# Expert rows placed as they come and read back in order, the first expert tiles begun before the last batches are routed, and an end in five chunks

## What is computed

```python
h = layernorm(x) * (1 + ca) + sa
x = x + ga * attention(h)          # 16 heads of 8, band of +-128 tokens
h = layernorm(x) * (1 + cb) + sb
logits = h @ gate                  # 8 experts
w, e = softmax over the two largest logits
x = x + gb * sum_k w[k] * ((silu(h @ w1[e[k]]) * (h @ w3[e[k]])) @ w2[e[k]])
```

## Time and profile before

| | us |
|---|---|
| median of three runs | 348.94 |
| the runs | 348.21 to 350.21 |
| the profiled execution | 349.13 |
| its span | 347.3 |
| TensorE busy | 277.7 |
| VectorE busy | 227.4 |
| ScalarE busy | 184.9 |
| GpSimd busy | 180.6 |
| mean granted clock of TensorE | 0.917 |

### The profile page before, as it was taken

One profiled execution on the slowest core, in us unless ns is written; L12 is line 12 of the kernel. 1 busy time (PEld: TensorE's weight loads), 2 busy tenths in 40 slices (PEclk: granted clock), 3 DMA queues, 4 the chain that ended last, 5 costly groups with the idle time before them and its releaser, 6 DMA issues. The chain is left out here.

```text
span 347.3 us, 6884 instructions
## 1 busy us (share of the span) xinstructions
PE 277.7 (80%) x2281; PEld 204.6 (59%) x2281; DVE 227.4 (65%) x573; ACT 184.9 (53%) x406; POOL 180.6 (52%) x269
## 2 busy tenths in 40 slices
PE   3568799999998999999854056999999999999200
PEld 2134354555554555555333035999999999999200
DVE  5657978888888799887437893555555555554064
ACT  7432477757675766667710104556665555555050
...
DMA packets 36243, 26.89 MB, mean 77 GB/s; under 512 B 4088, under 2 KB 31752, under 8 KB 36208
## 3 DMA queue, kind: packets, MB, share of 16 engines
...
## 5 line engine op out<-in xcount | busy, mean ns | idle before, releaser
L819 DVE TENSOR_REDUCE negm<-psA 128x4 f32<-128x1024 f32 x64 | 78.2, 1223 | 14.2 <-PE psA L1141 13.1
L428 ACT ACTIVATE probs<-psB 128x512 f32<-128x512 f32 x128 | 71.1, 593 | 21.4 <-PE psB L1163 21.1
L589 POOL TENSOR_SCALAR_AFFINE_SELECT probs<-probs 128x512 f32<-128x512 f32 x64 | 39.1, 634 | 42.2 <-ACT probs L428 42.2
L700 POOL DMA_INDIRECT y_d<-kd,sca_idx x39 | 45.3, 1162 | 22.9 <-ACT kd L497 22.9
L1297 PE MATMUL psA<-kd,probs 128*128 128x128 f32 x416 | 53.1, 284 | 0.0
L1297 PEld LDWEIGHTS psA<-kd,probs 128*128 128x128 f32 x416 | 51.1, 201 | 0.0
L1138 PE MATMUL psA<-kd,qs 96*128 96x512 bf16 x128 | 47.6, 395 | 1.7 <-DVE negm L819 1.5
L695 POOL DMA_INDIRECT kd<-h_d,gat_idx x39 | 38.2, 980 | 18.5 <-PE psO L1289 9.8
L1163 PE MATMUL psB<-qs,kd 98*128 98x256 bf16 x256 | 45.1, 273 | 1.5 <-ACT probs L428 1.0
L1307 PE MATMUL psM<-probs,kd 128*128 128x128 f32 x312 | 41.3, 275 | 0.4 <-ACT kd L497 0.4
L1307 PEld LDWEIGHTS psM<-probs,kd 128*128 128x128 f32 x312 | 37.9, 192 | 0.6 <-DVE kd L1030 0.6
...
## 6 DMA issues: line engine op xcount, KB each, us to landing
...
probs<-y_d SPq DMA_DIRECT2D x8, 256.0 KB, 5.0
h_d<-h SPq DMA_DIRECT2D x8, 128.0 KB, 1.9
out_dram<-probs SPq DMA_DIRECT2D x4, 256.0 KB, 2.3
...
```

The costliest lines, as they stand in the source:

```text
L428: nc.scalar.activation(probs[:, kt, n % PRING], psB[:, kt, :].rearrange("p (h q) -> p h q", h=H2), ACT.Exp).then_inc(s["exped"], 1)
L589: nc.gpsimd.affine_select(out=u, in_=u, compare_op=ALU.is_ge, fill=0.0, base=0, pattern=[[0, 2 * H2], [-sign, P]], channel_multiplier=sign ...
L700: pool.indirect_dma_start(y_d, bass.IndirectOffsetOnAxis(ap=sca_idx[:, n:n + 1], axis=0), ys[:, r], None).then_inc(scattered[r], 16)
L819: nc.vector.tensor_reduce(negm[:, b % 2, :, :, j], psA[:, n % 2].rearrange("p q (h k) -> p q h k", h=H2), AX.X, ALU.max, negate=True).then ...
```

## The change

- Every expert has a region of rows in DRAM (xs_d), as large as it could need. The place of a row is its rank within its expert plus the region's start, so it is known as soon as the ranks of its batch are. VectorE computes it per batch (`place_rows`), and GpSimd writes the rows there (`put_rows`, four indirect writes a batch, 520 bytes a row: 128 channels, the row of y_d that the result goes to, and its weight). A copy of h2 for the second choice is made by a transfer (`copy_h2`). Selection matrices, the inversion and the gathers are gone.
- Rows never written are blanks; they are written once at the start, only in front of each region and in a few dummy tiles (`fill_blanks`).
- The tile list is made in two parts. The first 13 of the 39 tiles (NEARLY) are full tiles of rows from batches 0 to 4 (EB = 5), since at least so many exist for any split; `early_list` is made in step 8. The other 26 come from `late_list`, made between tiles 5 and 6.
- SyncE loads a tile's rows with one plain transfer (`load_xs`, a ring of five) and w2 of the tile's expert straight from its input (`load_w2`, a ring of three), each behind a register read. The resident array of w2 and its copies on VectorE are gone. Rings for up products are two instead of three; results have a ring of six.
- The steps end with step 8. The tail of batches 5 to 7 stands between the tiles 0 to 5, on each engine.
- ScalarE applies the row's weight while it copies the result. The end has five chunks (4, 4, 4, 2, 2 tiles of tokens); SyncE loads first choices and ScalarE's queue second ones, 2 KB or 1 KB a partition; VectorE alone adds, gates and adds x.

```diff
...
+    XRING = 5
+    PAYRING = 3
+    ENDS = (0, 4, 8, 12, 14, 16)
+    YRING = 6
+    W = C + 2
+    EB = 5
+    NEARLY = -(-(TOPK * L * EB - E * (P - 1)) // P)
...
+            def load_w2(n):
+
+                if n >= TRING:
+                    sp.wait_ge(s["y_ps"], n - TRING + 1)
+                e = sp.value_load(tile_e[0:1, bass.ds(n, 1)], min_val=0, max_val=E - 1)
+                sp.dma_start(w2_t[:, n % TRING].rearrange("p (k c) -> p k c", c=C),
+                             w2[bass.ds(e, 1)].rearrange("e (k p) c -> p (e k) c", p=P)).then_inc(w2_in[n % TRING], 16)
+
...
+                if n >= XRING:
+                    sp.wait_ge(*result_down(n - XRING))
+                row = sp.value_load(tile_row[0:1, bass.ds(n, 1)], min_val=0, max_val=XROWS - P)
+                sp.dma_start(xs[:, n % XRING], xs_d[bass.ds(row, P), :]).then_inc(xs_in[n % XRING], 16)
...
+            sp.wait_ge(s["list_ready"], 2)
+            sp.wait_ge(s["scoresB"], 2 * NPAIR * B)
+            for n in range(TRING):
+                load_w2(n)
+            for done, count in xs_put_by(EB):
+                sp.wait_ge(done, count)
+            for n in range(XRING):
+                load_xs(n)
+            copy_h2(B - 2)
+            for n in range(NTILE):
+                if n + TRING < NTILE:
+                    if n + TRING == NEARLY:
+                        sp.wait_ge(s["list_ready"], 4)
+                    load_w2(n + TRING)
+                if n + XRING < NTILE:
+                    if n + XRING == NEARLY:
+                        sp.wait_ge(s["list_ready"], 4)
+                        sp.wait_ge(s["blanked"], 32)
+                        for done, count in xs_put_by(B):
+                            sp.wait_ge(done, count)
+                    load_xs(n + XRING)
+                if n == 2:
+                    copy_h2(B - 1)
+
+            for n in range(NTILE - YRING, NTILE):
+                sp.wait_ge(*result_down(n))
+            for i, (lo, hi) in enumerate(zip(ENDS, ENDS[1:])):
+                sp.dma_start(y01[:, 0, lo:hi], y_t[:, 0, lo:hi]).then_inc(y_in[i], 16)
...
+            def y_copy(n):
                 act.wait_ge(s["y_ps"], n + 1)
-                if not first(turn):
-                    act.wait_ge(scattered[r], 16 * turn)
-                nc.scalar.copy(ys[:, r], psY).then_inc(s["y_ready"], 1)
...
+            for i, (lo, hi) in enumerate(zip(ENDS, ENDS[1:])):
+                act.dma_start(y01[:, 1, lo:hi], y_t[:, 1, lo:hi]).then_inc(y_in[i], 16)
...
+            def put_rows(b, k, t):
+
+                r = b % PAYRING
+                pool.wait_ge(s["dest_ready"], 3 * b + 3)
+                if k == 1:
+                    pool.wait_ge(h2_copied[r], 16 * (b // PAYRING + 1))
+                pool.indirect_dma_start(xs_d, bass.IndirectOffsetOnAxis(ap=dest[:, b, k, t:t + 1], axis=0),
+                                        pay[:, r, k, t], None).then_inc(xs_put[r], 16)
...
                 for j in range(NPAIR):
+                    if 5 <= step < B and j >= 4:
...
                     if j == 3 and has(step - 3):
                         ln2_rstd(step - 3)
                     if j == 1 and has(step - 3) and step - 3 < B - 1:
...
+            put_rows(3, 1, 1)
+            put_rows(4, 0, 0)
+            pad_term(B - 1)
+            put_rows(4, 0, 1)
+            x1_sum(B - 2)
+            put_rows(4, 1, 0)
+            ln2_rstd(B - 2)
+            put_rows(4, 1, 1)
+            h2_scale(B - 2)
+            h2_shift(B - 2)
             for n in range(NTILE):
...
+                if n == 5:
+                    weights_pow(B - 1)
+                    put_rows(B - 3, 1, 1)
+                if n == 6:
+                    put_rows(B - 2, 0, 1)
+                if n == 7:
+                    put_rows(B - 2, 1, 1)
+                if n == 8:
+                    put_rows(B - 1, 0, 1)
+                if n == 9:
+                    put_rows(B - 1, 1, 1)
                 scatter(n)
-
-            for i in range(3):
-                tt = slice(NT // 4 * i, NT // 4 * (i + 1))
-                pool.wait_ge(s["comb_ready"], i + 1)
-                nc.gpsimd.tensor_tensor(outb[:, tt], comb[:, tt], x_sb[:, tt], ALU.add).then_inc(s[f"out_ready{i}"], 1)
+                if n == 4:
+                    put_rows(B - 3, 1, 0)
+                if n == 5:
+                    put_rows(B - 2, 0, 0)
+                if n == 6:
+                    put_rows(B - 2, 1, 0)
+                if n == 7:
...
+            def place_rows(b):
+
+                dve.wait_ge(s["rank_ps"], b + 1)
+                if b >= 2:
+                    dve.wait_ge(s["dest_ready"], 3 * b - 3)
+                nc.vector.tensor_tensor(
+                    picked[:, b % 2], pick[:, :, 2 * b:2 * b + 2],
+                    rank_at(b).rearrange("p (o t e) -> p o t e", o=1, e=E).broadcast_to([P, TOPK, 2, E]), ALU.mult).then_inc(s["rank_read"], 1)
+                nc.vector.tensor_copy(pay[:, b % PAYRING, :, :, C:C + 1].rearrange("p k t o -> p k (t o)").bitcast(I32),
...
+            def early_list():
+
+                dve.wait_ge(s["count_ps"], 1)
+                up_to(0, count_at(EB - 1))
+                list_done(nc.vector.tensor_scalar(jump[:], upto[:, 0, E:], -float(P), float(CAP), ALU.mult, ALU.add))
+                tile_list(0, NEARLY, jump[:])
...
+                    if j == 0 and step == B:
+                        place_rows(3)
+                        logits_copy(4)
+                    if j == 2 and step == B:
+                        top2(4)
+                    if j == 4 and step == B:
+                        place_rows(4)
+                        early_list()
...
+            w1_copy(1, 1)
+            ln2_stats(B - 2)
+            normalise_attn(B - 1)
+            ln2_normalise(B - 2)
...
-            n = NT // 4
-            for i in range(4):
...
-                dve.wait_ge(s[f"y_in{i}"], 32)
-                for j in range(n * i, n * i + n):
-                    dve.wait_ge(s["y0_scaled"], j + 1)
-                    ins = nc.vector.scalar_tensor_tensor(out=comb[:, j], in0=y01[:, 1, j], scalar=wts[:, 3, j:j + 1], in1=y01[:, 0, j],
-                                                         op0=ALU.mult, op1=ALU.add)
-                step_done(ins)
+                    if n + 2 == NEARLY:
+                        dve.wait_ge(s["list_ready"], 4)
+                    w1_copy(n + 2, (n + 2) % TRING)
+                if n == 1:
+                    gate_attn(B - 1)
+                    x1_last(B - 1)
+                    ln2_stats(B - 1)
+                if n == 2:
+                    place_rows(B - 3)
+                    ln2_normalise(B - 1)
+                    h2_last(B - 1)
+                if n == 3:
+                    logits_copy(B - 2)
...
+            for i, (lo, hi) in enumerate(zip(ENDS, ENDS[1:])):
+                tt = slice(lo, hi)
+                dve.wait_ge(y_in[i], 32)
+                step_done(nc.vector.tensor_tensor(comb[:, tt], y01[:, 0, tt], y01[:, 1, tt], ALU.add))
                 v = comb[:, tt].rearrange("p (b t) c -> p b t c", t=2)
-                ins = nc.vector.tensor_tensor(v, v, mod_sb[:, n * i // 2:n * (i + 1) // 2, 3:4, :].broadcast_to([P, n // 2, 2, C]), ALU.mult)
...
-                    ins.then_inc(s["comb_ready"], 1)
-                else:
-                    step_done(ins)
-                    nc.vector.tensor_tensor(outb[:, tt], comb[:, tt], x_sb[:, tt], ALU.add).then_inc(s["out_ready3"], 1)
...
+                        rank_alone(step - 5)
                     if j == 1 and has(step - 3):
...
                         scores_B(prev, j, 0)
-                    if j == 6 and step <= B and has(step - 4):
+                    if j == 6 and step < B and has(step - 4):
                         logits(step - 4)
+                    if j == 0 and step == B:
+                        logits(4, 3)
...
+                if n + 1 < NTILE:
+                    up(n + 1, (n + 1) % TRING)
+                if n + 2 < NTILE:
+                    xs_T(n + 2)
+                if n == 0:
+                    attn_T(B - 1)
+                if n == 1:
+                    project_out(B - 1)
+                    h2_T(B - 2)
+                if n == 2:
+                    rank_alone(B - 3)
+                if n == 3:
+                    logits(B - 2)
+                    h2_T(B - 1)
+                if n == 4:
+                    logits(B - 1)
+                    rank_alone(B - 2)
+                if n == 5:
+                    rank_alone(B - 1, count=True)
+                down(n, n % TRING)
 
 
...
```

591 lines of the change are left out of this document (315 added, 276 removed).

## The result

| | before | after |
|---|---|---|
| median of four runs, us | 349.48 | 359.56 |
| the runs | 348.21 to 350.21 | 355.04 to 360.02 |
| the profiled execution, its span | 349.13, 347.3 | 359.48, 357.7 |
| ratio, 95% interval | | 1.026 [1.017, 1.035] |

The changed kernel is slower, where 342.2 and a range of 331 to 351 had been forecast. Run again later, beside other kernels, it took 356.32 (352.08 to 357.67), a ratio of 1.015 [1.008, 1.022]. A median is of all runs of a kernel, and a ratio leaves out those over 1.5% above the fastest of theirs.

The account below looks back on a forecast made before the run. TensorE was taken as 99.5% busy in the expert tiles but working only 11.9 of 34.6 us before them. Terms -17.2 + 8.6 + 3.7 + 1.0 - 3.0 = -6.9 from 349.13 gave 342.2 us, range 331 to 351.

Parts of the forecast that it names:

- blanks at nothing: Start: memset and 1 MB of blank writes cost nothing, covered by GpSimd's waiting and replaced w2 loads; +2.3 us without cover.
- Steps 5 to 7: Attention steps: row placement and a subtraction on VectorE cost 1.0 us a step, +3.0 us, bounds 0 and +4.2.
- Step 8: Last attention step: logits, ranks and placement delay batch 5's projection, row writes push the last mask; +2.9 us, bounds 0 and +5.
- the fifth starts 4 x 1.39 + 1.96 + 0.1 = 7.6 later: Lead-in: GpSimd's fifth row write starts 7.6 us after the last mask, at 188.6, giving first product at 195.1, 17.2 earlier.
- The register read at 0.36 us: SyncE before row loads: a register read costs 0.36 us; at the skill's 600 ns the sum would be 0.5 more.
- Tiles 0 to 6: First expert tiles: VectorE's tail work of batches 5 to 7 delays them, +8.6 us, bounds +2.7 and +11.
- late rows: Tile 13: its loads wait for the last row write behind tile 8's scatter; +3.7 us, bounds 0 and +6.
- The clock: Two TensorE pauses near 4 us may drop the clock and slow the products behind; +1.0 us, bounds 0 and +4.
- Steady tiles: Later expert tiles: unchanged at 2.79 us each, TensorE having the same 25 products, with w2 now from HBM.
- Rival 3: Expert tiles: the ring of row buffers becomes the bound, period 3.3 us, 30 tiles add 15.3, 357.5 us; chance 0.12.
- The end: After the last product: combination starts sooner and costs less, smaller last store; -3.0 us, bounds -5 and 0.
- rival 2: Waits eat the gain: steps 5 to 8 at upper bounds add 3.3, clock 3.0; 348.5 us, no change; chance 0.10.

Follow-up runs that it names:

- experiment 2: Changed kernel with the rank products of steps 5 to 7 at the front of the step and read before VectorE's row maxima; 351.85 us, ratio 1.010.
- 10: Changed kernel with all reorderings (lead-in, late list split, late writes first), plus row writes of steps 5 to 7 spread over pairs 2 to 5; 338.53 us, ratio 0.973.
- experiment 3: Changed kernel with batch 5 normalised before batch 4's rows are placed in step 8, and most of the tile list made later; 356.39 us, ratio 1.020.
- 1: Changed kernel with GpSimd's last two row writes of batch 4 moved ahead of the sum and power of batch 6; 353.96 us, ratio 1.010.
- experiment 16: Changed kernel with GpSimd adding x in the first four of the end's five chunks; 364.57 us in one run, last product to end 22.10 us.

## Why the prediction was wrong

- *Start to batch 2, nothing forecast; +3.1.* 2.5 of it are there at the projection of batch 0. It comes at 75.66, and in the other profiles, with hardly an instruction moved ahead of it, between 72.57 and 77.20. So the blanks don't cost it, and "blanks at nothing" stands: nine of the profiles with the same blanks show it at 73.12 to 73.45, the kernel before at 73.14. Why some runs lose 2 to 4 us here is open (last section).
- *"Steps 5 to 7 ... I take 1.0 us a step: +3.0, bounds 0 and +4.2"; +10.8.* This is the step that failed. It counted the new operations at their durations and asked what GpSimd and VectorE had room for. It did not ask who waits for the read of the ranks, though the projection's psM is the bank that they are written to. That wait is 5.5 us with the low clock behind it (experiment 2), and 7.1 in most other profiles. A second cause was mis-sized: operations at 0.2 us, which beside GpSimd's take up to three times as long; 1.5 us come back when the writes are spread (10). The other 3.8 over the kernel before were not taken apart; they are near the bound of 4.2 for added work.
- *"Step 8: +2.9"; +5.1.* The low clock made 1.4 of it (19.3 against 17.9). In the rest is a wait that I had not looked for: placement and list stand ahead of the layer norm of batch 5, and the list was not in the term at all (2.3, experiment 3).
- *"the fifth starts 4 x 1.39 + 1.96 + 0.1 = 7.6 later"; 10.2.* The two operations between the writes were priced at what they take, 0.73 and 0.70; each waits for a chain through TensorE and VectorE, 1.23 and 2.08 us. Without them the lead-in is 4.6 shorter (1). Behind the write the forecast held: landing 2.41 against 2.5, and 4.1 to the first product against 4.0. Its parts were others: SyncE issued 0.8 us after the landing, not 0.36, and the first product waits for the rows of tile 1 too, whose load is issued 1.1 behind that of tile 0.
- *The register read at 0.36 us.* Between two loads on SyncE stand 0.76 us. The read itself (TENSOR_LOAD, 39 of them) takes 0.26 to 0.32, and the rest are small register instructions. The Trainium skill (DMA: Bandwidth & Descriptors, "Latency and other measured facts") has 600 ns as a floor for the read; these reads are shorter, and what the path pays is more, so neither that figure nor the row from ScalarE gave the price.
- *Tiles 0 to 6 +8.6, late rows +3.7.* Right in mechanism and place, and near in size. The gate product of tile 6 ended 29.2 us after the first product (forecast 31.7), and its down products at 31.3, which is +7.3, 1.0 of it the low clock. The wait at tile 13 was 3.98 (3.7), in part by luck: the last write stood at 43.1 (44.3) and took 4.3 us to land, not 2.5.
- *"The clock: +1.0, bounds 0 and +4"; 5.3.* 24 products behind each wait took 2.7 and 2.6 us longer. That is 4.3 over the term, and tiles 0 to 6 took 1.3 less than theirs: this is the tile phase's miss.
- *Steady tiles unchanged, ring no bound.* 2.79 us a tile to the end, with w2 from HBM, TensorE 99% busy. Rival 3 is refuted.
- *"The end: -3.0"; -4.7.* VectorE was done 13.0 us after the first load's issue (forecast 12.9), because two errors cancel: its first operation came after 4.3 us, not 3.5, and it worked 8.8, not 9.4. From its last operation to the end it is 2.3 instead of 4.5, where I had 0.4 for the smaller store. The store gave 0.5; 1.8 came from GpSimd's last instruction, which had ended the kernel before and was in no term (experiment 16).
- *"In the last step ... ScalarE is busiest".* The row shows TensorE at 11.53 of 13.30 us and ScalarE at 10.57. No term hangs on it.
- *Rivals and signs.* None of the rivals is what happened. The nearest in kind is rival 2, steps 5 to 8 longer, but it stopped at +9.2 and at the old time; they took +15.9. That is past the 9 us which the prediction itself gave as a sign of being wrong. The slower outcome had a chance of 0.12, for another reason.

Of the 17.3 us between forecast and span, 12.6 lie in the three stretches ahead of the first tile, 3.1 at the start and 3.4 in the tiles; the end gave 1.7 back.
